# Two tiles join one block later, a fifth bias buffer, and the packed rows' share made in the mean's tile

## The reference

```python
valid = sequence_ids < emb_table.shape[0]           # (1024, 200)
safe_ids = jnp.where(valid, sequence_ids, 0)
seq_emb = emb_table[safe_ids] * valid[..., None]    # (1024, 200, 512)
denom = jnp.maximum(valid.sum(axis=1, keepdims=True), 1.0)
user_repr = seq_emb.sum(axis=1) / denom             # (1024, 512)
logits = user_repr @ proj_w + proj_b                # (1024, 12500)
```

## Time and profile before

| what | us |
|---|---|
| median of 3 runs | 637.64 |
| lowest and highest | 637.17, 637.92 |
| the profiled execution's own time | 636.47 |
| its span, first to last instruction | 634.7 |
| TensorE busy with products | 609.6 (96% of the span) |
| VectorE busy | 408.0 (64%) |
| ScalarE busy | 145.3 (23%) |
| GpSimd busy | 230.7 (36%), all of it in the first 320 us or so |

### The profile page before, as it was taken

How to read it: one execution, slowest core, us unless ns; L and a number is a source line. 1 busy time by engine, 2 the same in 40 slices (tenths; PEclk the granted TensorE clock), 3 DMA queues, 4 the chain that set the end, 5 groups by cost and what they waited for, 6 DMA issues and landing times.

```text
span 634.7 us, 7598 instructions
## 1 busy us (share of the span) xinstructions
PE 609.6 (96%) x2602; PEld 478.6 (75%) x2602; DVE 408.0 (64%) x723; ACT 145.3 (23%) x161; POOL 230.7 (36%) x227
## 2 busy tenths in 40 slices
PE   1989899999999999999999999999999999999997
PEld 0347568787777777788888888888888888888886
DVE  7988978899879798797885553332333333344442
ACT  8916425141141131300200221111001111111210
POOL 5777878777755667565560000000000000000000
PEclk9988999999999999999999999999999999999999
DMA  9979999999998989798892498445455455556632
GB/s 312 387 255 350 378 395 364 374 318 342 303 326 290 294 293 300 233 324 254 254 334 90 126 291 277 137 141 171 169 177 176 165 178 177 187 186 204 216 125 103
DMA packets 77703, 158.31 MB, mean 249 GB/s; under 512 B 9287, under 2 KB 65042, under 8 KB 77658
## 3 DMA queue, kind: packets, MB, share of 16 engines
q1 hardware_dynamic: 60378, 110.30, 51.1%
q0 software_dynamic: 17280, 47.47, 22.8%
HBM read 115.70 MB, written 51.20 MB: 263 GB/s over the span
## 4 chain that ended last, share of the span: by engine, by line
PE 77%; DVE 14%; issue 4%; DMA 3%; DVEq 0%; ACT 0%; POOL 0%; POOLq 0%
PE acc L845 72%; DVE sums L561 6%; DVE w_lo L625 3%; PE turned L794 3%; DMA rows<-in_L_rec_emb_table_dram,index 3%; DVE key L518 1%; PE turned L786 1%; DVE top L514 1%; PE acc L850 1%; DVE stage L640 1%; DVE sums L558 0%; DMA ids_sb<-in_r_sequence_ids_dram 0%; PE turned L766 0%; DVE count L652 0%; ACT w_hi L422 0%
## 5 line engine op out<-in xcount | busy, mean ns | idle before, releaser
L353 POOL DMA_INDIRECT rows<-in_L_rec_emb_table_dram,index x208 | 220.9, 1062 | 92.0 <-issue 57.6
L640 DVE TENSOR_TENSOR stage<-acc,bias_sb 128x500 f32<-128x500 f32 x162 | 109.3, 676 | 181.3 <-PE acc L845 181.1
L845 PE MATMUL acc<-w_hi,mean_hi 128*128 128x500 f32 x800 | 224.5, 402 | 0.8 <-ACT mean_hi L438 0.8
L845 PE MATMUL acc<-w_hi,mean_lo 128*128 128x500 f32 x800 | 214.5, 390 | 0.4 <-DVE mean_lo L612 0.2
L845 PE MATMUL acc<-w_lo,mean_hi 128*128 128x500 f32 x800 | 214.7, 390 | 0.0
L845 PEld LDWEIGHTS acc<-w_hi,mean_lo 128*128 128x128 f32 x800 | 150.8, 189 | 32.2 <-DVE mean_lo L612 1.2
L845 PEld LDWEIGHTS acc<-w_lo,mean_hi 128*128 128x128 f32 x800 | 150.7, 188 | 31.4
L845 PEld LDWEIGHTS acc<-w_hi,mean_hi 128*128 128x128 f32 x800 | 150.2, 189 | 31.9 <-issue 4.3
L561 DVE SCALAR_TENSOR_TENSOR sums<-rows,mask,sums 128x512 f32<-128x512 f32 x165 | 124.1, 752 | 17.2 <-issue 8.2
L422 ACT ACTIVATE w_hi<-w_raw 128x2000 fp32r<-128x2000 f32 x39 | 72.9, 1874 | 233.5 <-PE acc L845 215.8
L625 DVE TENSOR_TENSOR w_lo<-w_raw,w_hi 128x1000 fp32r<-128x1000 f32 x74 | 85.3, 1194 | 11.7 <-ACT w_hi L422 11.7
(11 more groups left out here) (106 smaller groups left out, 190.1 us busy)
## 6 DMA issues: line engine op xcount, KB each, us to landing
out_dram<-stage SPq DMA_DIRECT2D x200, 250.0 KB, 3.8
w_raw<-in_L_rec_proj_w_dram SPq DMA_DIRECT2D x39, 1000.0 KB, 7.4
bias_sb<-in_L_rec_proj_b_dram SPq DMA_DIRECT2D x39, 250.0 KB, 4.5
raw_at_hi<-in_L_rec_proj_w_dram SPq DMA_DIRECT2D x4, 1000.0 KB, 11.9
rows<-in_L_rec_emb_table_dram,index POOLq DMA_INDIRECT x208, 6.0
raw_at_lo<-in_L_rec_proj_w_dram SPq DMA_DIRECT2D x3, 1000.0 KB, 14.5
stage<-in_L_rec_proj_w_dram SPq DMA_DIRECT2D x1, 1000.0 KB, 26.0
ids_sb<-in_r_sequence_ids_dram SPq DMA_DIRECT2D x1, 700.0 KB, 4.3
```

The source lines that it names most:

```text
L353: return pool.indirect_dma_start(out=dst, out_offset=None, in_=table, in_offset=bass.IndirectOffsetOnAxis(ap=column, axis=0), bounds_check ...
L640: dve.tensor_tensor(stage[:, g % STAGE, r - stores[g][0]], acc[:, r % BANKS, 0:BW], bias_sb[:, i % BIAS], ALU.add).then_inc(s_moved_by_dve, 1)
L845: last = nc.tensor.matmul(bank, first, second, start=part + k == 0, stop=part == 2 and k == K - 1 and not by_act[r])
```

## The change

It has three edits.

1. **The order at two joins.** At tile 1's and tile 2's join, the tiles that are already there take the new block before the joining tile begins to catch up. For tile 1, block 10 of tile 0 moves from unit 14 to unit 10, and the four catching-up units from 10 to 13 to 11 to 14; `joined[1]` is 11 in place of 10. For tile 2, block 14 of tiles 0 and 1 moves from units 26 and 27 to 22 and 23, and `joined[2]` is 24 in place of 22. From unit 28 on the order is as before, and so are `joined[3]` and all later ones. What hangs on `joined` moves with it: TensorE's packed product and columns go from unit 8 to 9 and from 20 to 22, the turned means, the shares, the lists and the slots by as much. `behind_others` keeps the columns of tiles 1 and 2 about where they were due; those of tile 3 start at unit 22 in place of 20 and end at 32 as before. VectorE's queue then has the drain of unit 21 in front of tile 2's mean, and that of 23 in front of tile 3's slots. The high and low halves of blocks 11 to 14 are due one unit later, those of 15 to 17 two units later.
2. **Five bias buffers** in place of four.
3. **No tile `rest_mean`.** The packed rows' share is written to `mean`, and the final sum reads it from there and writes it in place. That frees 2 KB in each partition, what the fifth bias buffer takes.

```diff
--- before.py
+++ after.py
@@ -24,11 +24,12 @@
     REST = SORTED - FAST
     REST_AT = 14
     LISTED = -(-FAST // TOP) * TOP
-    RAW, SPLIT, BIAS, ROWS, PLACED, BANKS = 2, 5, 4, 12, 2, 6
+    RAW, SPLIT, BIAS, ROWS, PLACED, BANKS = 2, 5, 5, 12, 2, 6
     CH = 2
 
     ON_PE, DIAGS = ((0, FAST), (18, FAST), (24, FAST)), 4
     RAW_MORE, MORE_LOADS = 2, 16
+    OTHERS_FIRST = 2
     FURTHER_BEHIND, LIST_FIRST_AT, BIAS_DUE = 20, 21, 3
     ACT_TILES, BOTH_TILES = 1, 5
     PART_AT = (0, 32, 64)
@@ -52,11 +53,15 @@
     LOADS = start[-1] + NB
     steps = []
     for q in range(LOADS):
-        for t in range(1, TILES):
+        for t in range(OTHERS_FIRST + 1, TILES):
             if JOIN[t] == q:
                 steps += [(x, t, 1) for x in range(start[t], q)]
         here = [t for t in range(TILES) if JOIN[t] <= q < start[t] + NB]
-        steps.append((q, here[0], len(here)))
+        if q in JOIN[1:OTHERS_FIRST + 1]:
+            steps.append((q, here[0], len(here) - 1))
+            steps += [(x, here[-1], 1) for x in range(start[here[-1]], q + 1)]
+        else:
+            steps.append((q, here[0], len(here)))
     units = [(q, first + m) for q, first, n in steps for m in range(n)]
     UNITS = len(units)
     assert UNITS == TILES * NB
@@ -89,12 +94,16 @@
     GATHER_LEAD = 5
     LATE_LOAD, REST_FIRST_AT, OPENED = 7, 18, SPLIT - 1
 
+    def behind_others(t):
+
+        return t if t <= OTHERS_FIRST else 0
+
     def column_due(c):
 
         t, j = divmod(c, FAST)
         if by_pe[c]:
             return joined[t] - 2
-        begin, end = joined[t - 1] - 2 if t > 1 else 0, joined[t] - SUM_AHEAD
+        begin, end = joined[t - 1] - 2 if t > 1 else 0, joined[t] - behind_others(t) - SUM_AHEAD
         return begin + (end - begin) * j // (dve_last[t] - FAST * t)
 
 
@@ -155,7 +164,6 @@
         value = sb("value", [P, 1], F32)
         rest_index = sb("rest_index", [P, TILES], U32)
         rest_rows = sb("rest_rows", [P, HID], F32)
-        rest_mean = sb("rest_mean", [P, HID], F32)
         rows = sb("rows", [P, ROWS, HID], F32)
         mean = sb("mean", [P, HID], F32)
         ident = sb("ident", [P, P], F32)
@@ -446,7 +454,7 @@
                 if t < len(ON_PE):
                     act.wait_ge(s_added, sum(len(x) for x in pe_columns[0:t + 1]))
                 act.wait_ge(s_rest, t + 1)
-                nc.scalar.activation(rest_mean[:], turned[:], ACT.Copy,
+                nc.scalar.activation(mean[:], turned[:], ACT.Copy,
                                      scale=inv_count[:, t:t + 1]).then_inc(s_rest_mean, 1)
 
             act.wait_ge(s_const, 1)
@@ -593,18 +601,18 @@
 
             def first_mean():
 
-                dve.tensor_scalar(rest_mean[:], sums[:], inv_count[:, 0:1], None, ALU.mult).then_inc(s_further_mean, 1)
+                dve.tensor_scalar(mean[:], sums[:], inv_count[:, 0:1], None, ALU.mult).then_inc(s_further_mean, 1)
                 dve.wait_ge(s_further_mean, 1)
                 dve.wait_ge(s_rest, 1)
                 dve.wait_ge(s_added, len(pe_columns[0]))
-                dve.scalar_tensor_tensor(mean[:], turned[:], inv_count[:, 0:1], rest_mean[:], ALU.mult,
+                dve.scalar_tensor_tensor(mean[:], turned[:], inv_count[:, 0:1], mean[:], ALU.mult,
                                          ALU.add).then_inc(s_mean, 1)
 
             def mean_of(t):
                 dve.wait_ge(s_summed, nth[dve_last[t]] + 1)
                 dve.wait_ge(s_turned, t)
                 dve.wait_ge(s_rest_mean, t)
-                dve.scalar_tensor_tensor(mean[:], sums[:], inv_count[:, t:t + 1], rest_mean[:], ALU.mult,
+                dve.scalar_tensor_tensor(mean[:], sums[:], inv_count[:, t:t + 1], mean[:], ALU.mult,
                                          ALU.add).then_inc(s_mean, 1)
 
             def mean_low(t):
```

## The result

The changed kernel takes 640.08 us, median of 6 runs (639.85 to 640.54), against 637.24 us for the kernel before in the same comparison: a ratio of 1.0045 (95% interval 1.0032 to 1.0057), 2.8 us slower. The forecast was 641.0 and slower. The two profiled executions differ by 3.4 us, 639.88 against 636.47, the sum that was worked out; the medians differ by a little less. Two executions among the experiments, one of 3448.27 us with tile 1's join alone and one of 869.47 us with all three joins, are left out of the ratios.

A forecast was written before the change was run, and what follows sets the result against it. The chain runs through VectorE from 99.61 us to mean(3) at 166.04 us, then TensorE to the end. Later mean(3), 1.91 us, plus clock, 1.5 us, gave 3.4 us, added to the median 637.64: 641.0 us, range 637.5 to 643.0.

The forecast's parts named there:

- Tile 1 on TensorE, 2.95 us ahead: At tile 1's join, unit 8 fits before the last column's rows land at 85.24, putting TensorE 2.95 us ahead.
- VectorE gains 0.37 us there: Block 11's low half starts at 99.24 instead of 99.61, a gain of 0.37 us; bounds 0 and 2.91 us.
- mean(2) held: At tile 2's join VectorE waits 1.6 us for ScalarE's share; mean(2) starts at 127.90 instead of 126.05.
- Tile 3's slots: The list, behind two more units, ends at 136.36; VectorE waits another 0.65 us and the slots start at 136.52.
- mean(3), 1.91 us later: VectorE starts tile 3's mean at 167.95 instead of 166.04, 1.91 us later.
- TensorE idle 5.87 us in front of it: TensorE reaches tile 3's join at 162.88 and its transposes start at 168.75: 5.87 us idle.
- The clock, 1.5 us: Behind the idle stretch before tile 3's transposes TensorE's clock falls, costing 1.5 us; bounds nothing and 2.9 us.
- The other edits at nothing: Share in the mean's tile and fifth bias buffer change nothing; 0.73 us more of bias loading on SP is hidden.
- (a): Rival: the clock falls at tile 1 too, units 9 and 10 losing up to 1.5 us: 642.5 us; chance 0.12.
- (b): Rival: no loss of clock at 168 us, leaving 639.5 us; chance 0.12.
- (c): Rival: VectorE's two new waits don't come, mean(3) stays, the change does nothing: 637.3 to 638.5 us; chance 0.20.
- (d): Rival: VectorE's 2.91 us of idle time before 99 us vanish, mean(3) starts 2.9 us earlier: 634.7 us; chance 0.14.

The follow-up runs named there:

- tile 2's earlier support: Changed kernel's order of units, with all that hangs on tile 2's join one unit earlier: 641.18 us, ratio 1.0061.
- the mean before the drain: The run of tile 2's earlier support, with mean(2) put in front of unit 21's drain in VectorE's queue: 640.62 us, ratio 1.0053.

## Why the prediction was right, step by step

- **Tile 1 on TensorE, 2.95 us ahead.** Right. The last column's rows came at the same time, and the list behind unit 11 stood 0.12 us behind where it had stood behind unit 10. Alone it is worth nothing, as the run with only that join showed.
- **VectorE gains 0.37 us there.** The low half of block 11 started at 99.29 where 99.24 was worked out. Right.
- **mean(2) held.** 127.92 where 127.90 was worked out, with ScalarE's share as its releaser. The last 1.49 us of it is idle time; 1.6 was expected.
- **Tile 3's slots.** 136.38 for 136.52. The wait was 0.28 us and not 0.65: VectorE's work in between took 8.18 us in place of 7.97, and the list ended at 136.33. The place was right, its idle part mis-sized.
- **mean(3), 1.91 us later.** 1.83 us: it started at 167.87 where 167.95 was worked out, and the transposes at 168.68, 1.84 us later. What was called 32.02 us of work also holds idle time of VectorE, 0.49 and 1.17 us in front of tile 3's columns before the change, 0.95 us in the changed kernel, so the agreement to 0.08 us is in part luck: without any of the edits to the order mean(3) lay 1.15 us later in one execution (167.19). The run with tile 2's join alone gave 4.4 us for mean(3) where 4.9 was worked out, by the same steps.
- **TensorE idle 5.87 us in front of it.** 5.82.
- **The clock, 1.5 us.** It fell; 1.73 us between transposes and list, and 1.5 us by the run that kept TensorE busy. That it falls was borne out: it fell in all seven executions with an idle stretch of 4.53 to 6.47 us in front of a tile's transposes, so the bound of nothing, from the row of the 0.79 us wait, is out for stretches of this length. The size was luck in part: the same instructions lost 1.37 to 2.47 us (table above). And the 1.45 us came from unit 0, in front of which, with the same last 0.78 us of waiting, the clock fell in only seven of the 14 profiled executions: unit 0 took 4.3 to 4.4 us there and 2.8 to 2.9 us in the other seven. The rule quoted from the Trainium skill ("TensorE: Matmul & The Clock Gate", Part 1, What's actually happening: throttled by default, released by activity) gave the right side here. By itself it doesn't say which waits lower the clock: 1.91 us for diagonals did in the kernel before, 2.12 us for the same in the run with only block 20's halves later did not.
- **The other edits at nothing.** Shown by the two runs that part them from the order. SP issued five bias loads in 3.93 us in place of four in 2.92 us, 1.01 us more and not 0.73, and it was hidden.
- **Rivals.** (a) The clock held at tile 1: TensorE waited there 0.77 us in two pieces; the rest of the 1.63 us lies inside the six columns before them, 5.84 us for 6 x 0.86 = 5.16 us of products. It can fall there: in the profiled execution of the run with tile 3's join alone it was low from 77.5 to 84.3, behind a wait of 2.53 us, and tile 2's list came 1.0 us later than in the kernel before (96.56 against 95.55). (b) is out by the clock's fall, (c) by the two holds and mean(3), (d) by the low half of block 11 at 99.29 and the hold at mean(2).

The term of the sum that was furthest off is the clock's, 1.5 us for a measured 1.73 us; mean(3)'s was 0.07 us too large. The two add up to 3.57 us, of which 3.39 us are left behind tile 4's join, so that the profiled pair gives 3.4. Against the medians the sum is overstated, 3.4 us for a measured 2.8 us, and the median of the kernel before came out at 637.24 and not 637.64: together the 0.9 us by which the forecast of 641.0 is too high. The first part lies within what single executions differ by at mean(3); no run settles it. One figure of the prediction is wrong by itself: 1.0 us off the wait or the clock gives 640.0 as the lower edge of the likeliest case, not 640.2. The measured 640.08 lies between the two.

Three later expectations failed, for one reason. At tile 2's earlier support, at tile 3's join alone and at all three joins I followed the queue to the next mean and not past it, or not through its own turn: a drain in front of a mean (1.45 and 3.47 us), a block's halves in front of the columns (4.35 and 5.59 us). A fourth, for the mean before the drain, missed by 1.1 us: the places were right, and the clock's fall cost 2.2 us.

## What to carry to other kernels

When two engines are nearly tied, work out for each semaphore between them where its producer moves to, in units of the producer's order, and whether the consumer's queue stands at it: one engine's gain of 2.95 us became 2.8 us of loss because 5.67 us of units were put ahead of two small products that the other engine needs. A gain at one join has to be carried through every later one; follow it until there is slack, and look in front of what was needed for work that could wait, such as a block's halves due 14 units early. Price an idle stretch of TensorE with the clock behind it, and try cheap products in its place to see that term alone.

## What the runs showed of the hardware that had not been expected

- The price of a fall of the clock isn't set by the length of the idle stretch: 1.73 us behind 5.82 us, 2.47 us behind 6.47 us, 1.4 us behind 4.75 us, 2.2 us behind 4.53 us, each over the same instructions. It was a little under half of the low stretch that lay on products (3.7, 5.4, 3.0 and 4.9 us).
- A wait that lowers the clock in one execution need not in another: the stand in front of unit 0 did in seven of 14, and 1.91 us for diagonals did where 2.12 us did not. Two waits of 1.09 and 0.41 us with products between them, and the ones of 0.54 and 0.23 us, lowered nothing.
- Products whose results nobody uses kept the clock up: 24 of them, 5.64 us, won 1.5 us by the medians. With 18 of them, 4.28 us, it was 2.7 us by the medians and 1.5 us by the profiled pair.
